# An order written by hand, twice: SP's DMAs in a gated delta-rule recurrence, and PE's work in the projection and routing behind it

## The reference

```
q, k, v = silu(short_conv(x @ Wq|Wk|Wv))          # 8 heads of 128, three k and v per head and token
beta, g = 2*sigmoid(x @ Wb), -exp(A_log)*softplus(x @ Wa + dt_bias)
per token: S *= exp(g); three times: S += beta * k (v - k.S); o = q.S
o = rms_norm(o) * rms_weight * silu(x @ Wg)
x = layernorm(x + o @ Wo)
x = layernorm(x + sum over the top 2 of 8 experts of share * (silu(gate * up) @ down))
```

## Time and profile before

| | us |
|---|---|
| median of 3 executions | 5214.37 (5207.93 to 5220.62) |
| the profiled execution, its span | 5212.94, 5211.1 |
| PE busy / DVE busy / ACT busy / POOL busy | 4387.1 / 3641.6 / 3283.0 / 1648.1 |
| mean granted TensorE clock, share of 2.4 GHz | 0.883 |
| stage 3, first load of a tile to the last scale | 4234 to 4505.5 |

### The profile page before, as it was taken

One profiled execution on the slowest core, in us unless ns is written; L12 is line 12 of the kernel. 1 busy time (PEld: TensorE's weight loads), 2 busy tenths in 40 slices (PEclk: granted clock), 3 DMA queues, 4 the chain that ended last, 5 costly groups with the idle time before them and its releaser, 6 DMA issues. The chain is left out here.

```text
span 5211.1 us, 149412 instructions
## 1 busy us (share of the span) xinstructions
PE 4387.1 (84%) x47876; PEld 3922.9 (75%) x47876; DVE 3641.6 (70%) x10194; ACT 3283.0 (63%) x9028; POOL 1648.1 (32%) x1615
## 2 busy tenths in 40 slices
PE   2999888888888888888888888999988966499992
PEld 1888777787787777777778778888888855388881
DVE  6898777677777776777777778888777732244445
ACT  3787766667666666666676667877766631165552
POOL 3444333333332333333333333443333312200004
PEclk6999988789888888888898899999889888699996
DMA  5232222222223233222222222322333223366664
GB/s 228 83 89 69 70 74 73 62 67 74 74 67 67 61 69 70 64 74 74 70 63 74 74 70 64 92 74 67 73 77 80 52 70 107 102 232 230 228 232 130
DMA packets 363273, 490.68 MB, mean 94 GB/s; under 512 B 94080, under 2 KB 308096, under 8 KB 343680
## 3 DMA queue, kind: packets, MB, share of 16 engines
q1 hardware_dynamic: 345744, 453.87, 30.2%
q0 software_dynamic: 6144, 16.79, 1.0%
q10 hardware_dynamic: 10608, 10.23, 0.6%
HBM read 352.02 MB, written 107.75 MB: 88 GB/s over the span
## 5 line engine op out<-in xcount | busy, mean ns | idle before, releaser
L1132 DVE SCALAR_TENSOR_TENSOR conv_acc<-bank,c_cur,conv_acc 128x256 f32<-128x256 f32 x2688 | 1256.6, 477 | 51.3 <-ACT conv_acc L952 39.2
L700 PE MATMUL bank<-x_cur,w_cur 128*128 128x259 f16 (+1 forms) x6144 | 884.0, 281 | 39.9 <-DVE v_rows L1120 26.3
L1327 POOL TENSOR_TENSOR squares<-kq_t 128x768 f32<-128x768 f32 x128 | 187.9, 1468 | 1871.1 <-ACT kq_t L963 1871.1
L1193 DVE CAST_PREDICATED xs_lev<-mask,bank 128x256 f16<-128x256 uint16 x1536 | 662.3, 431 | 90.0 <-PE bank L764 69.9
L1001 ACT ACTIVATE inv<-bank 128x256 f16<-128x256 f32 x1536 | 606.0, 395 | 173.8 <-PE bank L776 171.2
L700 PEld LDWEIGHTS bank<-x_cur,w_cur 128*128 128x128 f16 (+1 forms) x6144 | 564.7, 100 | 131.7 <-DVE v_rows L1120 27.2
L1010 ACT ACTIVATE invt<-bank 128x256 f16<-128x256 f32 x1280 | 511.2, 399 | 50.1 <-PE bank L788 48.9
L952 ACT ACTIVATE conv_acc<-bank,c_cur 128x256 f32<-128x256 f32 x896 | 426.9, 476 | 152.5 <-PE bank L700 145.9
L1340 POOL TENSOR_TENSOR n_t<-n_t,cst 128x512 f32<-128x512 f32 x256 | 326.2, 1274 | 590.3 <-DVE n_t L1160 590.3
L832 PE MATMUL bank<-w_sol,k_rows 128*128 128x128 f32 x2048 | 494.8, 326 | 3.0 <-ACT w_sol L1020 2.7
L800 PE MATMUL bank<-inv,n_high 128*128 128x128 f16 x1024 | 173.9, 249 | 361.5 <-ACT invt L1010 361.5
(11 more groups left out here) (241 smaller groups left out, 11630.8 us busy)
## 6 DMA issues: line engine op xcount, KB each, us to landing
w_cur<-w_parts_scratch SPq DMA_DIRECT2D x128, 1024.0 KB, 7.0
ew<-e_parts_scratch SPq DMA_DIRECT2D x117, 896.0 KB, 6.0
x_cur<-x_parts_scratch SPq DMA_DIRECT2D x128, 259.0 KB, 7.0
x_slots<-no_rows SPq DMA_DIRECT2D x128, 256.0 KB, 3.2
e_parts_scratch<-e_pair SPq DMA_DIRECT2D x96, 224.0 KB, 2.8
o_rows<-w_sol SPq DMA_DIRECT2D x512, 32.0 KB, 3.7
y_scratch<-y_buf SPq DMA_DIRECT2D x128, 128.0 KB, 2.4
y_in<-y_scratch SPq DMA_DIRECT2D x32, 512.0 KB
```

The lines of the kernel that those rows point to most:

```text
L700: last = mm(bank[i % 2][:, 0:PW], w_cur[k.i % 2][:, wp, kt, c * P:(c + 1) * P].bitcast(BF16 if wp else F16), x_cur[k.i % 2][:, xp, kt, 0:P ...
L1132: v.scalar_tensor_tensor(acc, bank[at % 2][:, i:i + TB], c_cur[k.i % 2][:, c, i:i + 1], acc, ALU.mult, ALU.add).then_inc(tap_step.sem if i ...
L1193: v.copy_predicated(half(xs_lev[g][l - 1][:], l, 0), half(mask4[:, l], l, 0).bitcast(U16), packed(halves(LEVX), l)).then_inc(x_kept.sem, 1)
```

## The change

SP's stream in the recurrence: `body` keeps only t_cur; the clearing and the y store become a function of their own, `outputs`; the order of a slot becomes body, load_next, move_outputs, outputs, pieces. In stage 3 there are four buffers for the loads instead of two; PE projects two tiles ahead and makes the logits of the tile before the one that it transposes; DVE's pick, PE's count and DVE's place come one, one and two tiles later; DVE's add waits in addition for the tile two before to have been scaled, because xr still has two buffers. ACT's and POOL's streams are as they were.

```diff
@@ SP in the recurrence
+                    def outputs(tb, head, new=True):
+                        n = B * H * tb + head
                         if new:
                             sp.dma_start(clear_rows[bass.ds(n * P, P), :], no_rows[:]).then_inc(cleared, 16)
                         d = n - STORED
...
                         for head in range(B * H):
                             body(tb, head)
-                            pieces(tb, head)
                             load_next(tb, head)
                             move_outputs(B * H * tb + head - 3, head - 3)
+                            outputs(tb, head)
+                            pieces(tb, head)
@@ SP in stage 3
-                if i >= 2:
-                    sp.wait_ge(outp, i - 1)
-                    sp.wait_ge(added, i - 1)
+                if i >= YD:
+                    sp.wait_ge(outp, i - YD + 1)
+                    sp.wait_ge(added, i - YD + 1)
+                sp.dma_start(y_in[i % YD][:], yv[b, tb, :, :, half * P:(half + 1) * P]).then_inc(y_ld[i % YD], 16)
+                sp.dma_start(x_in_b[i % YD][:], x_rows[i * P:(i + 1) * P, :]).then_inc(y_ld[i % YD], 16)
@@ PE
             project(0)
+            project(1)
             for i in range(NTT):
-                if i + 1 < NTT:
-                    project(i + 1)
-                route(i)
-                if i % GRP == 2 and i > GRP:
+                if i + 2 < NTT:
+                    project(i + 2)
+                turn_rows(i)
+                if i:
+                    logits_of(i - 1)
+                if i % GRP == 3 and i > GRP:
                     count(i // GRP - 1)
+            logits_of(NTT - 1)
@@ DVE
+                if i >= 2:
+                    dve.wait_ge(x2_made, i - 1)
...
-                if i % GRP == 2 and i > GRP:
+                if i % GRP == 3 and i > GRP:
                     pick(i // GRP - 1)
-                if i % GRP == 4 and i > GRP:
+                if i % GRP == 6 and i > GRP:
                     place(i // GRP - 1)
```

More of the change, by code:

```diff
@@ L658, in _ @@
                         body(0, head)
-                        pieces(0, head)
                         load_next(0, head)
                         move_outputs(B * H * 0 + head - 3, head - 3)
+                        outputs(0, head)
+                        pieces(0, head)
                     with sp.Fori(1, NTB - 1) as tb:
@@ L664, in _ @@
                             body(tb, head)
-                            pieces(tb, head)
                             load_next(tb, head)
                             move_outputs(B * H * tb + head - 3, head - 3)
+                            outputs(tb, head)
+                            pieces(tb, head)
                     for head in range(B * H):
                         body((NTB - 1), head)
-                        pieces((NTB - 1), head)
                         if head + 1 < B * H:
@@ L673, in _ @@
                         move_outputs(B * H * (NTB - 1) + head - 3, head - 3)
+                        outputs((NTB - 1), head)
+                        pieces((NTB - 1), head)
                     for i in range(max(STORED, 4)):
-                        body(NTB, i, new=False)
                         move_outputs(NIT + i - 3, i - 3)
+                        outputs(NTB, i, new=False)
                     for i in range(2):
@@ L1403, in experts @@
     NG = NTT // GRP
+    YD = 4
     wo = sb("wo", [P, H, D], F32)
     x2 = sb("x2", [P, NTT, D], F32)
-    y_in = [sb(f"y_in{i}", [P, H, P], F32) for i in range(2)]
-    x_in_b = [sb(f"x_in{i}", [P, D], F32) for i in range(2)]
+    y_in = [sb(f"y_in{i}", [P, H, P], F32) for i in range(YD)]
+    x_in_b = [sb(f"x_in{i}", [P, D], F32) for i in range(YD)]
     xr = [sb(f"xr{i}", [P, D], F32) for i in range(2)]
@@ L1455, in experts @@
     b_small = sem("b_small")
-    y_ld = [sem("y_ld0"), sem("y_ld1")]
+    y_ld = [sem(f"y_ld{i}") for i in range(YD)]
     (outp, added, st_made, ag_made, rs_made, x2_made, x2_turn, x2t_kept, logit, logit_kept) = map(sem, (
@@ L1474, in _ @@
                 b, tb, half = i // (NTT // B), (i % (NTT // B)) // 2, i % 2
-                if i >= 2:
-                    sp.wait_ge(outp, i - 1)
-                    sp.wait_ge(added, i - 1)
-                sp.dma_start(y_in[i % 2][:], yv[b, tb, :, :, half * P:(half + 1) * P]).then_inc(y_ld[i % 2], 16)
-                sp.dma_start(x_in_b[i % 2][:], x_rows[i * P:(i + 1) * P, :]).then_inc(y_ld[i % 2], 16)
+                if i >= YD:
[3 more added lines that the diff above has]
+                sp.dma_start(x_in_b[i % YD][:], x_rows[i * P:(i + 1) * P, :]).then_inc(y_ld[i % YD], 16)
         @block.gpsimd
@@ L1526, in project @@
             def project(i):
-                pe.wait_ge(y_ld[i % 2], 32 * (i // 2 + 1))
+                pe.wait_ge(y_ld[i % YD], 32 * (i // YD + 1))
                 if i == 0:
@@ L1532, in project, with turn_rows @@
                 for h in range(H):
-                    last = mm(bank[i % 2][:, 0:D], y_in[i % 2][:, h], wo[:, h], start=(h == 0), stop=(h == H - 1))
+                    last = mm(bank[i % 2][:, 0:D], y_in[i % YD][:, h], wo[:, h], start=(h == 0), stop=(h == H - 1))
                 last.then_inc(outp, 1)
-            def route(i):
+            def turn_rows(i):
                 pe.wait_ge(x2_made, i + 1)
@@ L1542, in route, with logits_of @@
                 last.then_inc(x2_turn, 1)
+            def logits_of(i):
                 pe.wait_ge(x2t_kept, i + 1)
@@ L1642, in _ @@
                 dve.wait_ge(outp, i + 1)
-                dve.wait_ge(y_ld[i % 2], 32 * (i // 2 + 1))
-                v.tensor_tensor(xr[i % 2][:], bank[i % 2][:, 0:D], x_in_b[i % 2][:], ALU.add).then_inc(added, 1)
+                dve.wait_ge(y_ld[i % YD], 32 * (i // YD + 1))
+                if i >= 2:
+                    dve.wait_ge(x2_made, i - 1)
+                v.tensor_tensor(xr[i % 2][:], bank[i % 2][:, 0:D], x_in_b[i % YD][:], ALU.add).then_inc(added, 1)
                 dve.wait_ge(added, i + 1)
```

## The result

The changed kernel takes 5036.21 us (median, 5033.26 to 5046.13), the kernel before 5211.15 in the same comparison (5154.57 to 5220.62): a ratio of 0.969 [0.9619, 0.976]. The profiled execution took 5033.34 us.

What follows compares the result with a forecast made beforehand. Bounds: the serial chain from x_cur in each recurrence slot, delayed by SP's earlier DMAs, then a four-engine loop per tile behind it. Terms -28 - 88 + 6 = -110 from 5212.94 give 5103 us; range 5070 to 5155.

Steps and rivals of the forecast that it cites:

- SP's order, the time freed: In the recurrence, x_cur leaves earlier once pieces, clearing and y store move behind it: 28 us credited.
- The slower rival: In the recurrence, pieces queued right behind o_rows delay its landing, 1.6 us a slot, 153 us, total 5256; chance 0.03.
- The recurrence gives nothing: Slots bound by the same loop whichever way SP starts, or DMA noise swallows the gain: total 5131; chance 0.12.
- SP's order, what it is worth: In the recurrence, the total gain from moving SP's DMAs: 28 us, with nothing for the moved DMAs.
- The bound of 45 us: Upper bound on the recurrence's gain, if the 448 KB of pieces also stand before x_cur in the DMA queue.
- ACT's wait for o_rows falls by 28: Sign of being right, in the recurrence: ScalarE's wait for o_rows falls from 442 us by some 28.
- The tile: Stage behind the recurrence: a tile at full clock becomes PE's own work, 4.45 us instead of 6.77.
- The picks: Choosing experts, three times inside the loop behind the recurrence: PE waits 4.2 us, then counts 0.8; 15 us together.
- Clock and late results behind scatters: Stage behind the recurrence: 18 us allowed, 6 for scatters and late results, 12 for PE at 1.2 GHz.
- The tail: After the last add, GpSimd's last scatter waits for the one before it: 6 us lost.
- Half clock: PE stays at 1.2 GHz through the stage behind the recurrence, tiles of 7.7 us, total 5183; chance 0.05.
- The last stage: Behind the last scatter's start nothing changes: experts' stage and the end as before, 0 us.

Runs made afterwards that it cites:

- f4: The changed kernel with the clearing and y store ahead of load_next again, only the weight pieces last: 5053.02 us, ratio 0.9709.
- e1: The kernel before with only SP's new order in the recurrence, the stage behind it as before: 5154.49 us, ratio 0.9888.
- e3: The changed kernel itself, run again unchanged in another comparison on another chip: 5081.27 us, ratio 0.9747.
- f1: The changed kernel with 16 more semaphore increments on SP ahead of x_cur in each slot: 5285.91 us, ratio 1.0154.
- f2: The changed kernel with 20 extra products that nobody reads on PE, where it stands still for the o_rows chain: 4909.61 us, ratio 0.943.
- f3: The changed kernel with both the 16 increments on SP and the extra products on PE: 5069.69 us, ratio 0.9739.
- e4: The changed kernel with move_outputs exchanged to stand ahead of load_next: 4400.95 us, ratio 0.8439.
- g3: The changed kernel with all of GpSimd's scatters held until the add of the last tile: 5085.39 us, ratio 0.977.

## Why the prediction was wrong

- **SP's order, the time freed: right.** 28 us credited, 26 measured from the tap to the square; x_cur leaves 0.2 to 0.4 us after the tap in every slot; it comes through one to one, as the step from the earlier trace rows said. The slower rival (pieces behind o_rows cost) falls with f4 and with the landings. "The recurrence gives nothing" falls with e1.
- **SP's order, what it is worth: wrong, and the step that failed.** The sum put down the time freed and nothing for what follows it. A shorter stand-still of PE leaves it longer at 2.4 GHz, which shortens the next part of the slot too: another 37 us (68 in e1's profile, 35 in e3's), shown by f1, f2 and f3. I had used this very rule against the picks, where 3 slow projections were at stake, and not in the 128 slots, where 900 us at the low clock lay in front of me. The Trainium skill (TensorE: Matmul & The Clock Gate, Part 1) has it that gaps between bursts bring the throttle back; the two windows above (1.00 and 0.70) and f2 agree. The bound of 45 us was wrong for the same reason: it held only causes on SP and in the queue.
- **"ACT's wait for o_rows falls by 28": wrong as a sign.** It fell by 7 (to 435), or 20 in e3. When the part ahead of the square gets shorter, ACT arrives there sooner as well; a total of idle time isn't a loss account.
- **The tile: right mechanism, mis-sized.** 4.45 predicted, 4.12 measured; I added durations that overlap. Thirty tiles: 10 us.
- **The picks: right place, too cheap.** 5 us each predicted, 6.3, 7.5 and 7.8 measured, since I had the slow projection behind each in another term. Together 22 against 15 us.
- **Clock and late results behind scatters: 18 us allowed,** none in the first profile beyond the picks, 20 in e3 (181.1 against 160.7). That the allowance fits e3 is partly luck: it gave 6 us to late results and 12 to slow projections, and in e3 the 20 us come on top of the slow projections behind the picks. For the forecast it was the second largest miss. From the add of tile 1 to that of tile 31 the first profile has 144.2 us: 30 x 4.12 = 123.6, 21.7 for the picks, 1 less for the first tiles. I had 166.
- **The tail: right in the first profile,** +5.8 against +6, and not in e3: there a late count holds DVE's place, GpSimd waits 4.28 us for it, and the last scatter starts 23.0 us behind the last add, +9.7.
- **Half clock: didn't come, and one reading was wrong.** I had PE at 1.2 GHz from 4356 to 4390 and two thirds busy. In these 34 us PE is busy for 27.5 and the granted clock is 0.65 in the mean, with stretches at both levels. The rival leaned on it.
- **The last stage: -9.3 that no step explains.** From the last scatter's start e3 takes 696.0 us, the kernel before 694.4; it is a property of that one profiled execution, cause open.

Together: 39 us missed in the recurrence, 21 in the stage behind it, 9 in the last, which is the 70 between -110 and -180. In e3's comparison the same change is worth 133 us and its time lies in my range; the step that failed, the recurrence's, failed there too (62 us against 28), and the less favourable stage behind hides it. Of the 41 us between the two profiles 20 lie in the stage with the scatters, 4 between its last add and the last scatter, 11 behind that and 6 ahead of the stage; why the two comparisons differ so is open.

## What to carry to other kernels

Where a stand-still recurs in every slot and the clock is below full, price a microsecond taken from it at more than one: here 1.7 (205 us for 122, f1) to 2.3 (60 for 26, e1, whose interval of 40 to 77 us makes it 1.5 to 3); look at the windows behind short and long stand-stills of the same kernel to find the factor. Before trimming what stands ahead of a group of DMAs, list for the one DMA that ends a wait when its data are ready and what is issued ahead of it: o_rows needed nothing of the four loads, and two exchanged calls were worth 680 to 731 us where the change was worth 133 to 175.

## What the runs showed of the hardware

- Products that nobody reads, put into a stand-still of some 3 us a slot, made the kernel 172 us faster (4909.61 against 5081.27), by the granted clock (0.97 against 0.90 in the windows).
- 16 semaphore increments on SP took 1.0 us: (156.3 - 34.4)/122.
- SP's issue of g_cur, 2 KB, took 3.11 us, that of w_cur, 1 MB, 0.61 (slot 59 of the changed kernel).
- An o_rows DMA of 32 KB landed 4.5 us after its issue when 1.3 MB of loads and three other o_rows had been issued in the 8 us before it (e3), and after 2.2 when they had not (e4); means of the last of four in 122 slots.
- GpSimd's indirect scatters beside PE, DVE and ACT made results reach other engines late (a projection that ended at 4260.13 was added at 4262.28; the longest such wait in e3 is 15.5 us) and cost the stage 23 us (181.1 in e3 against 158.5 in g3); the first profile of the changed kernel has no such wait.
- float32 transposes and 8-column logits behind a projection cost 0.42 us together, though their modelled times sum to 0.89.
